# Image 0's first normalisation and projections ahead of image 1's, fold products in the convolution's drain, rounding of queries on GpSimd

## The reference

```python
x = x + conv_attention(groupnorm(x))      # 7x7 local attention, batch norm over (0,2,3), relu
t = tokens(x)                             # [2, 1024, 128]
t = t + attention(layernorm(t))           # 8 heads; only the diagonal of the softmax is used
t = t + ffn(layernorm(t))                 # 2 of 8 experts per image, then a layer norm
```

## Time and profile before

| | |
|---|---|
| time, median of 3 | 413.36 us (413.03 to 414.14) |
| profiled execution | 413.38 us, span 411.6 us |
| mean granted TensorE clock | 0.998 |
| PE busy | 394.4 us (96%) |
| DVE busy | 311.7 us (76%) |
| ACT busy | 296.7 us (72%) |
| POOL busy | 96.5 us (23%) |
| chain that ended last | PE 81%, DVE 8%, ACT 8%, issue 3% |

### The profile page before, as it was taken

The page is one execution under the profiler, slowest core; times in us unless marked ns, Lnnn a source line. Parts: engine busy times, 40 slices in busy tenths (PEclk is TensorE's granted clock), DMA queues, the critical chain, the costliest instruction groups (busy, mean ns, idle before and its releaser), DMA issues.

```text
span 411.6 us, 5629 instructions
## 1 busy us (share of the span) xinstructions
PE 394.4 (96%) x1906; PEld 302.4 (73%) x1906; DVE 311.7 (76%) x701; ACT 296.7 (72%) x577; POOL 96.5 (23%) x94
## 2 busy tenths in 40 slices
PE   8899899999999999999999899999999999997995
PEld 3579795578777888888886688888888766645772
DVE  2798936668888988988899788898899265557745
ACT  1566664558788998999888899899898301457980
POOL 7300013111221520220220242662420000124015
PEclk9999999999999999999999999999999999999999
DMA  7990000000000000000000190000000000000002
GB/s 275 383 304 1 2 2 0 2 1 0 2 1 2 1 0 2 1 0 2 0 0 2 37 375 2 0 0 2 1 2 0 0 2 0 2 0 1 1 2 102
DMA packets 5262, 15.51 MB, mean 38 GB/s; under 512 B 690, under 2 KB 1906, under 8 KB 4978
## 3 DMA queue, kind: packets, MB, share of 16 engines
q1 hardware_dynamic: 4802, 14.19, 9.5%
q10 hardware_dynamic: 432, 0.97, 0.6%
HBM read 14.08 MB, written 1.08 MB: 37 GB/s over the span
## 4 chain that ended last, share of the span: by engine, by line
PE 81%; DVE 8%; ACT 8%; issue 3%; POOLq 0%; POOL 0%; ACTq 0%; DVEq 0%
PE ps L1061 12%; PE ps L1063 12%; PE ps L1062 12%; PE ps L1045 11%; PE ps L1153 7%; PE ps L810 4%; DVE nmax_all L1504 3%; PE ps L990 2%; PE ps L940 2%; PE ps L997 2%; PE ps L910 2%; PE ps L981 2%; PE ps L961 1%; ACT exps L691 1%; ACT qT_hi L681 1%
## 5 line engine op out<-in xcount | busy, mean ns | idle before, releaser
L1504 DVE TENSOR_REDUCE nmax_all<-ps 128x1 f32<-128x1024 f32 x128 | 156.7, 1224 | 8.2 <-PE ps L1063 6.6
L691 ACT ACTIVATE exps<-ps,nmax_all 128x1024 bf16<-128x1024 f32 x128 | 143.4, 1133 | 17.9 <-DVE diag_all L1509 17.3
L1061 PE MATMUL ps<-qT_hi,kT_hi 128*128 128x512 f32 x256 | 104.7, 409 | 2.8 <-ACT exps L691 1.3
L1063 PE MATMUL ps<-qT_hi,kT_lo 128*128 128x512 f32 x256 | 99.8, 390 | 0.0
L1062 PE MATMUL ps<-qT_lo,kT_hi 128*128 128x512 f32 x256 | 99.7, 390 | 0.0
L475 POOL TENSOR_TENSOR qT_lo<-xq,qT_hi 128x1024 fp32r<-128x1024 f32 x16 | 38.3, 2395 | 168.7 <-ACT xq L681 168.7
L1061 PEld LDWEIGHTS ps<-qT_hi,kT_hi 128*128 128x128 f32 x256 | 48.0, 188 | 16.5 <-ACT exps L691 2.9
L1045 PE MATMUL ps<-xn,wqkv 128*128 128x342 f32 (+3 forms) x256 | 58.2, 379 | 0.1
L1062 PEld LDWEIGHTS ps<-qT_lo,kT_hi 128*128 128x128 f32 x256 | 48.1, 188 | 10.9 <-issue 0.2
L1063 PEld LDWEIGHTS ps<-qT_hi,kT_lo 128*128 128x128 f32 x256 | 48.1, 188 | 10.3
L1045 PEld LDWEIGHTS ps<-xn,wqkv 128*128 128x128 f32 x256 | 42.6, 189 | 11.7 <-issue 0.9
(11 more groups left out here) (214 smaller groups left out, 552.1 us busy)
## 6 DMA issues: line engine op xcount, KB each, us to landing
xs_first<-a_store SPq DMA_DIRECT2D x4, 512.0 KB, 5.3
xs_second<-a_store SPq DMA_DIRECT2D x4, 512.0 KB, 8.4
wqkv<-laid_qkv_weights SPq DMA_DIRECT2D x1, 1536.0 KB, 6.2
wvT<-laid_qkv_weights_T SPq DMA_DIRECT2D x1, 1536.0 KB, 9.5
xq<-laid_x_queries SPq DMA_DIRECT2D x2, 512.0 KB, 6.3
xk<-laid_x_keys SPq DMA_DIRECT2D x2, 512.0 KB, 7.7
x<-in_x SPq DMA_DIRECT2D x1, 1024.0 KB, 12.4
w<-in_L_ffn_W SPq DMA_DIRECT2D x1, 1024.0 KB
```

Source lines behind the costliest of these rows:

```text
L691: a.activation(exps[:, n % 2, :], slot(job_slot(("score", u, n))), ACT.Exp, bias=nmax_all[:, col:col + 1], accum_out=sum_all[:, col:col + ...
L1061: mm(tgt, keys_hi, qT_hi[:, u % 2, at], start=True, stop=False)
L1063: last = mm(tgt, keys_lo, qT_hi[:, u % 2, at], start=False, stop=True)
L1504: v.tensor_reduce(nmax_all[:, col:col + 1], slot(place), AX_X, ALU.max, negate=True)\
```

## The change

Six things change.

1. Fold products 0 to 3 move into steps 16 to 19 of the convolution, in front of the outputs, in place of the fillers of steps 17 to 19. The vector products follow the drain in one run, then fold products 4 and 5. The waits for `w0`, `wvT` and the last maximum move to steps 16 and 18.
2. ScalarE's load of the table for square roots moves from step 16 to behind the drain. The load for exponentials moves from ahead of unit 0's evacuations to behind them. The fillers behind `bn_root` go.
3. TensorE's order of LN[0] becomes: means 0, 1; variances 0, 1; mean 2; spreads 0, 1; queries of unit 0; mean 3; keys of unit 0; variances 2, 3; ten fillers instead of fifteen. The second half's variances go to bank 7.
4. VectorE's order follows: the last residual of image 1 between centrings 0 and 1, the copies of the vector products behind centring 1, centrings 2 and 3 behind the multiplications of chunks 0 and 1, the second reciprocal behind the keys' remainder of unit 0.
5. GpSimd squares chunks 2 and 3 (a new semaphore `late_square`) ahead of its first query remainder, and lays the diagonals of chunks 2 and 3 after it.
6. From unit 1 on ScalarE evacuates queries only into `queries_full`, and GpSimd makes `qT_hi` of it by a copy that rounds, waits for it, and subtracts as before.

```diff
@@ GpSimd
+            for c in (2, 3):
+                pool.wait_ge(LN[0]["centred"], c + 1)
+                at = slice(c * 512, (c + 1) * 512)
+                g.tensor_tensor(squares[:, at], centred[:, at], centred[:, at], ALU.mult).then_inc(late_square, 1)
...
                 pool.wait_ge(q_full, 3 * u + 3)
+                if u:
+                    g.tensor_copy(qT_hi[:, u % 2, :], queries_full).then_inc(q_hi, 1)
+                    pool.wait_ge(q_hi, 3 + u)
                 g.tensor_tensor(qT_lo[:, u % 2, :], queries_full, qT_hi[:, u % 2, :].bitcast(F32), ALU.subtract)\
...
                 queries_remainder(u)
+                if u == 0:
+
+                    pool.wait_ge(LN[0]["rstd"], 2)
+                    lay_diagonal(0, 2)
+                    lay_diagonal(0, 3)
@@ ScalarE
-                if s == CONV_TILES:
-                    load_table(ACT.Sqrt)
+
+            load_table(ACT.Sqrt)
...
             root(0, 0, 7)
-            square(0, 2)
-            square(0, 3)
-            root(0, 1, 0)
-            load_table(ACT.Exp)
...
-                for dst, signal in ((qT_hi[:, u % 2, :], q_hi), (queries_full, q_full)):
+                whole = ((queries_full, q_full),)
+                for dst, signal in whole if u else ((qT_hi[:, u % 2, :], q_hi),) + whole:
...
             evacuate_keys(0)
+            root(0, 1, 7)
+            load_table(ACT.Exp)
@@ TensorE
                     for job in (("q", 2 * CHUNKS - 1), ("v", 2 * CHUNKS - 1)):
                         taken(*job)
+                    pe.wait_ge(w0_in, 16)
+                    pe.wait_ge(wvT_in, 16)
+                if s == CONV_TILES + 2:
+                    pe.wait_ge(cm_sb, CONV_TILES)
...
-                    if s > CONV_TILES:
-                        keep_warm(7, 2)
+                    if s >= CONV_TILES:
+                        fold_products(s - CONV_TILES)
...
+            for h in range(HEADS):
+                mm(bank(VB_BANK, 3 * h, 3 * h + 3), w0[:, h, :], bqkv[:, :, h], start=True, stop=True)
+            mm(bank(VB_BANK, 3 * HEADS, 3 * HEADS + E), mean_w[:, :], b2_all, start=True, stop=True).then_inc(vb_ps, 1)
+            fold_products(4)
+            fold_products(5)
+            for signal, count, times in ((bn_aff, 1, 3), (bn_relu, 1, 3), (bn_relu, 2, 2)):
...
             channel_means(0, 1, x1, "mean", 4)
-            pe.wait_ge(x1_ready, 6)
-            channel_means(0, 2, x1, "mean", 5)
-            pe.wait_ge(f_m_sb, 5)
-            channel_means(0, 3, x1, "mean", 6)
             pe.wait_ge(f_m_sb, 6)
             variances(0, 0, 7, 0)
             variances(0, 0, 7, 1)
-            pe.wait_ge(vb_sb, 1)
-            pe.wait_ge(b2_centred, 1)
-            variances(0, 1, 0, 2)
-            variances(0, 1, 0, 3)
+            pe.wait_ge(x1_ready, 6)
+            channel_means(0, 2, x1, "mean", 5)
...
             project("queries", 0)
+            channel_means(0, 3, x1, "mean", 6)
             pe.wait_ge(LN[0]["out"], 2)
-            pe.wait_ge(f_m_sb, 4)
             project("keys", 0)
+            pe.wait_ge(LN[0]["sqrt"], 1)
+            variances(0, 1, 7, 2)
+            variances(0, 1, 7, 3)
             pe.wait_ge(LN[0]["centred"], 4)
-            keep_warm(5, 3)
+            keep_warm(5, 2)
             pe.wait_ge(q_full, 2)
-            keep_warm(5, 5)
+            keep_warm(5, 2)
             pe.wait_ge(k_hi, 2)
-            keep_warm(5, 7)
+            keep_warm(5, 6)
+            pe.wait_ge(LN[0]["sqrt"], 2)
@@ VectorE
+            centre(0, 0, x1, 3)
+            first_residual(1, 2)
+            centre(0, 1, x1, 4)
+            dve.wait_ge(vb_ps, 1)
...
             reciprocals(0, 0)
             lay_diagonal(0, 0, LN[0]["diagonal"])
             lay_diagonal(0, 1, LN[0]["diagonal"])
             normalise(0, 0, 3, xn)
             normalise(0, 1, 4, xn)
-            reciprocals(0, 1)
-            lay_diagonal(0, 2, LN[0]["diagonal"])
-            lay_diagonal(0, 3, LN[0]["diagonal"])
+            centre(0, 2, x1, 5)
+            centre(0, 3, x1, 6)
...
             keys_remainder(0)
+            reciprocals(0, 1)
```

More of the change, by code:

```diff
@@ L287, in build @@
         h_ps, h_full, h_sb, h_lo, y_ps = (sem(n) for n in ("h_ps", "h_full", "h_sb", "h_lo", "y_ps"))
-        b2_ps, b2_centred, w2_mean_ready, w2_centred = (sem(n) for n in (
-            "b2_ps", "b2_centred", "w2_mean_ready", "w2_centred"))
+        b2_centred, w2_mean_ready, w2_centred = (sem(n) for n in (
+            "b2_centred", "w2_mean_ready", "w2_centred"))
         xn_hi_ready, xn_lo_ready = sem("xn_hi_ready"), sem("xn_lo_ready")
+        late_square = sem("late_square")
         last_diagonal = sem("last_diagonal")
@@ L524, in _ @@
                 pool.wait_ge(LN[2]["rstd"], 1 if c < 2 else 2)
-                g.tensor_tensor(diagonal[:, c, :].rearrange("p (i n) -> p i n", i=4), ident_of_tiles, rstd_of(c),
-                                ALU.mult).then_inc(LN[2]["diagonal"], 1)
+                lay_diagonal(2, c)
             for c in range(3):
@@ L888, in step_job, with fold_products @@
                 project_job(*STEP_JOB[s])
+            def fold_products(n):
+                if n >= 4:
+                    pe.wait_ge(f_m_sb, n - 3)
+                for m in range(4 * n, 4 * n + 4):
+                    last = mm(bank(FOLD_AT[n], m % 4 * D, (m % 4 + 1) * D), wvT[:, m // 3, m % 3, :], w0[:, m // 3, :],
+                              start=True, stop=True)
+                last.then_inc(f_m_ps, 1)
             pe.wait_ge(mask_in, 16)
@@ L947, in _ @@
                         mean_shift(1, j)
-            pe.wait_ge(w0_in, 16)
             pe.wait_ge(cols_in, 16)
[L951 to L976, removed]
+            for h in range(HEADS):
[4 more added lines that the diff above has]
+            for signal, count, times in ((bn_aff, 1, 3), (bn_relu, 1, 3), (bn_relu, 2, 2)):
                 pe.wait_ge(signal, count)
@@ L986, in variances @@
                 chunks = LN_PARTS[k][part]
-                pe.wait_ge(LN[k]["square"], c + 1)
+                if k == 0 and part == 1:
+                    pe.wait_ge(late_square, c - 1)
+                else:
+                    pe.wait_ge(LN[k]["square"], c + 1)
                 for i in range(4 * c, 4 * c + 4):
@@ L1092, in _ @@
             pe.wait_ge(LN[0]["out"], 1)
-            pe.wait_ge(f_m_sb, 3)
+            pe.wait_ge(b2_centred, 1)
             project("queries", 0)
+            channel_means(0, 3, x1, "mean", 6)
             pe.wait_ge(LN[0]["out"], 2)
-            pe.wait_ge(f_m_sb, 4)
             project("keys", 0)
+            pe.wait_ge(LN[0]["sqrt"], 1)
+            variances(0, 1, 7, 2)
+            variances(0, 1, 7, 3)
             pe.wait_ge(LN[0]["centred"], 4)
-            keep_warm(5, 3)
+            keep_warm(5, 2)
             pe.wait_ge(q_full, 2)
-            keep_warm(5, 5)
+            keep_warm(5, 2)
             pe.wait_ge(k_hi, 2)
-            keep_warm(5, 7)
+            keep_warm(5, 6)
+            pe.wait_ge(LN[0]["sqrt"], 2)
             for g, (kind, u, n) in enumerate(JOBS):
@@ L1419, in _, with first_residual @@
                 .then_inc(bn_aff, 1)
[L1421 to L1425, removed]
-            dve.wait_ge(x_in_sem, 16)
[L1427 to L1438, removed]
+            dve.wait_ge(x_in_sem, 16)
+            def first_residual(b, n):
+                lo, hi, first = THIRDS[n]
+                x_at, x1_at = (whole[:, b * HW:(b + 1) * HW].rearrange("p (j r) -> p j r", r=RUN)[:, first::3, :]
+                               for whole in (x, x1))
+                third = conv_e[:, b, lo * RUN:hi * RUN].rearrange("p (j r) -> p j r", r=RUN)
+                if b == 0:
+                    dve.wait_ge(bn_relu, n + 1)
+                    inst = v.tensor_tensor(x1_at, x_at, third, ALU.add)
+                else:
+                    dve.wait_ge(bn_scaled, n + 1)
+                    inst = v.scalar_tensor_tensor(x1_at, third, 0.0, x_at, ALU.max, ALU.add)
+                inst.then_inc(x1_ready, 1)
+            for n in range(3):
+                first_residual(0, n)
+            first_residual(1, 0)
+            first_residual(1, 1)
             def centre(k, c, source, n):
@@ L1466, in normalise @@
                 inst.then_inc(LN[k]["out"], 1)
-            for c in range(4):
-                centre(0, c, x1, 3 + c)
+            centre(0, 0, x1, 3)
+            first_residual(1, 2)
+            centre(0, 1, x1, 4)
+            dve.wait_ge(vb_ps, 1)
+            v.tensor_copy(vb[:, :, :], bank(VB_BANK, 0, 3 * HEADS).rearrange("p (h j) -> p j h", j=3)).then_inc(vb_sb, 1)
+            v.tensor_tensor(b2c[:, :], b2_all, bank(VB_BANK, 3 * HEADS, 3 * HEADS + E), ALU.subtract)\
+                .then_inc(b2_centred, 1)
             reciprocals(0, 0)
```

4 lines of the change are left out of this document (3 added, 1 removed).

## The result

The changed kernel took 409.84 us (median of 4; 408.94 to 410.23) against 413.19 us (412.97 to 414.14), a ratio of 0.9895, interval 0.9866 to 0.9924. The four runs were 408.94, 409.47, 410.20 and 410.23, so the median lies between two pairs and no run took it. Forecast were 409.4 us and a range of 407.9 to 411.8. In a second session it took 410.31 against 413.39, ratio 0.9922 (0.9892 to 0.9952). The profiled execution took 410.20 us, span 408.4, granted clock 0.995.

What follows compares the result with a forecast made beforehand. TensorE was taken to bound the attention loop and, from 50 us on, nearly all the chain ahead of it. Gains of 3.2 us before the first score and 0.8 in the loop took 413.38 to 409.4 us, range 407.9 to 411.8.

Steps and rivals of the forecast that it cites:

- signs of being wrong: Residuals above 0.5 us, first score waiting for qT_lo or kT_lo, q_split stall each unit, clock below 1 between 58 and 72.
- The forecast's own case: Whole kernel: 3.2 us gained ahead of the loop and 0.8 in it, giving 409.4 us; chance 60%.
- Drain: End of convolution: four fold products of 1.00 us, TensorE bound; last evacuation at 57.8 instead of 56.07, 1.7 later.
- Batch norm: After the drain: ScalarE's table load and two fold copies hold the root, which starts at 60.6 instead of 59.01.
- First mean: After batch norm: fillers and third residual meet at 63.9; first mean starts at 64.4 against 65.77, 1.4 gained.
- a rival: TensorE sparse from 57.8 to 72: clock at 1.2 GHz from 60 adds 9 us, giving 418; chance 4%.
- the bound I set on it: Full clock held through 376 to 380 with TensorE busy 2.54 of 4 us; a fall needs a sparser stretch.
- Residuals beside GpSimd: In batch norm: GpSimd's three scalings beside VectorE's first residuals cost 0.4 us, between nothing and 0.9.
- My 0.9: Upper bound for residuals beside scalings in batch norm: all six run one after another from 61.65 to 64.85.
- Normalisation: Image 0: root 0 at 68.7, spread at 70.05, queries of unit 0 at 71.9 instead of 75.77, 3.9 gained.
- Queries to first score: Ahead of the loop: TensorE's queue of 8.3 us, its fillers ending last, puts the first score at 80.2; 3.2 gained.
- The loop: Attention loop: stalls of 0.53 at 124.24 and 0.30 at 227.21 go; 0.8 us gained, between 0 and 1.5.

Runs made afterwards that it cites:

- the undoing: The change with fold products 0 to 3 back behind the drain, two vector products after each, and fillers in the drain as before: 409.64 us.
- the version that closes it: The change with ScalarE's copies of fold banks 0 to 3 moved inside the drain: 408.24 us.

## Why the prediction was right, and where not

The time, the direction and the range held: 409.84 for 409.4, and 410.31 in the second session. Of the signs of being wrong that were written down, three came true: single residuals of 0.72 and 0.76 us, a first score that waits for the keys' remainder, and a clock below 1 between 58 and 72. The forecast's own case, with the clock up and a drain that begins where it did before (50.06 for 50.07), is the trace with fillers among the vector products: last evacuation at 57.52 for 57.8, root at 60.37 for 60.6, first mean at 63.99 for 64.4, first query projection at 72.02 for 71.9, first score at 80.77 for 80.2. So the path was read rightly but for one link near its end. The parts, in the changed kernel's own trace, whose drain began 0.47 earlier than that of before, so that 0.47 is to be taken off the forecast times:

**Drain.** Forecast: bound by TensorE, last evacuation at 57.8, so 57.3. Measured 57.06. Right, and the undoing showed that it is a price: the root came 1.5 to 1.9 earlier without it.

**Batch norm.** Root at 60.6, so 60.1; measured 59.91, held by the table load and the two fold copies, as said. What I did not do was to ask whether the copies had to stand there. ScalarE had 1.08 us of waiting in each of the last three steps of the drain.

**First mean.** Forecast 64.4, so 63.9; measured 64.94. Here a rival came true in small. I had given the clock 4% and priced it at 9 us, from a fall that lasts to 72; it fell, for three microseconds, and cost 1.6 on these products (3.63 for 2.0) and 0.7 to 1.3 on the kernel (410.2 for 409.47 and 408.94). The step that failed is the bound I set on it: that the clock holds wherever TensorE is no sparser than in 376 to 380. Measured, 56.86 to 59.59 had 2.08 of 2.73 us busy, denser than that by its busy share, and still the clock fell. A busy share from a stretch of wide matmuls is no bound for one of three-column ones followed by a gap. That the gap is needed for it is shown by the version that closes it and leaves TensorE's products as they are (clock up in its trace, six runs within 0.45 us); the fillers (410.31 to 409.34) agree. Why some runs of the change escape stays open.

**Residuals beside GpSimd.** I took 0.4 for it. The three adds took 1.63 us for 1.47, so it was 0.16; GpSimd's three scalings took 3.11 us for 1.85, and nobody waited for them. My 0.9 had VectorE wait for every scaling; in the trace GpSimd did most of the waiting. The first mean was set by the fillers anyway.

**A scaling I had left out.** The prediction weighed only VectorE instructions with two SBUF inputs, and so missed the small scaling of w2_mean, which reads one. It cost 1.28 us of its own and 0.35 to 0.47 on the first score. The page "SBUF — State Buffer" of the Trainium skill, section "Who interferes with whom", lists `tensor_scalar` among the instructions that can enter a two-port mode, if their operands allow it, and then exclude GpSimd; the trace agrees, 1.46 beside GpSimd's subtraction and 0.12 without. It was on the page that I cited, two bullets further.

**Normalisation.** From the first mean to the first query projection 7.5 us were forecast and 7.79 measured (64.94 to 72.73 in the chain).

**Queries to first score.** 8.3 forecast, 8.75 measured: the ten fillers end near 81.15, as computed, and the score follows the remainder, held by the scaling, 0.34 later. The square on GpSimd took 1.04 for my 1.2.

**The loop.** 0.8 forecast, 1.26 measured. I had added up the idle times of two rows, 0.53 at 124.24 and 0.30 at 227.21. What a vanished stall gives back is read from the next weight load, set against its counterpart: the loop's lead grows by 0.67 at 124.24 (where the load had waited 0.69), by 0.36 at 227.21 (0.30), and by 0.19 near 219, where a load in front of the projections waited 0.46 for an exponential and now 0.27. That is the 1.2. The largest stall behind an exponential is still there, and the one for the turned weights as well, as I had said of the latter. Before, then changed, in pairs:

```profile
219.19 1.45 PEld L1045 LDWEIGHTS ps<-xn,wqkv 128*128 128x128 f32 x8 [0.46 <-ACT exps L691]
216.31 1.46 PEld L1050 LDWEIGHTS ps<-xn,wqkv 128*128 128x128 f32 x8 [0.27 <-ACT exps L706]
...
223.50 0.50 PE L1061 MATMUL ps<-qT_hi,kT_hi 128*128 128x512 f32 x1 [0.75 <-ACT exps L691]
220.61 0.50 PE L1066 MATMUL ps<-qT_hi,kT_hi 128*128 128x512 f32 x1 [0.73 <-ACT exps L706]
...
229.43 0.50 PE L1066 MATMUL ps<-qT_hi,kT_hi 128*128 128x512 f32 x1 [1.09 <-ACT a_rows L723]
```

**Where the gain is.** In the faster group of runs: rounding 413.05 to 411.8, 1.25; the new order of the normalisation with its companions (later table loads, fewer fillers, squares on GpSimd, interleaved vector products) 411.8 to 409.6, 2.2, not taken apart further; the products in the drain, 0.7 lost with the clock down (410.3) and 0.2 to 0.7 gained with it up (409.47 and 408.94). That the forecast sum was so near owes something to chance. In the profiled execution the first mean came 1.0 late, the normalisation took 0.3 more and the stretch to the first score 0.45, while the loop gave 0.46 more and the opening 0.47; together 0.8, which is 409.4 to the measured 410.2. And the median of 409.84 is nearer only because two of four runs seem to have escaped the fall.

## What to carry to other kernels

Work moved into another engine's idle time pays only if the engine that must clear its result also has its slot there: the fold products lost time in most runs until ScalarE's copies moved with them. When fillers are taken away, look at what is left between them: small matmuls and a gap in one place cost about 1 us here, more than the 0.65 us of fillers that mend it. And give every instruction that runs beside GpSimd, however small, its place in the list of the path; 16 numbers a partition held the first score.

## What was not expected of the hardware

- The granted clock fell from 2.4 to 1.2 GHz behind 1.85 us of three-column products, a small product and 0.65 us of idleness, and came back after three microseconds of fold products. With the products followed at once by wide ones it did not fall in the trace, nor by their times in any of six runs; with 2.54 of 4 us busy elsewhere it did not fall either. The same instructions with the same gap fell in some runs and not in others.
- A VectorE `TENSOR_SCALAR` over 128x16 from SBUF to SBUF took 1.46 us beside a GpSimd `TENSOR_TENSOR` and 0.12 to 0.18 without, while `SCALAR_TENSOR_TENSOR` with one input from PSUM and `TENSOR_REDUCE` from PSUM ran beside it at full speed.
- Where VectorE's two-input additions met GpSimd's scalings, VectorE lost 11% (1.63 us for 1.47) and GpSimd 68% (3.11 for 1.85).
- GpSimd copies 1024 float32 columns with rounding in 1.04 us, and multiplies 512 columns by themselves in 1.04, where a subtraction of two tiles takes 2.4 for 1024.
